# Expert results scattered to the tokens' order inside the expert loop, and one chunk of scans moved a layer on

## The reference

```python
logits = x @ router_w
expert_idx = jnp.argmax(logits, axis=-1)
score = jax.nn.sigmoid(jnp.max(logits, axis=-1))
xs = x * score[:, None]
for e in range(n_experts):          # 8 experts
    m = (expert_idx == e)[:, None]
    xe = jnp.where(m, xs, 0.0)
    h = jax.nn.silu(xe @ gate_w[e]) * (xe @ up_w[e])
    out = out + jnp.where(m, h @ down_w[e], 0.0)
shared = jax.nn.silu(x @ shared_gate_w) * (x @ shared_up_w) @ shared_down_w
return (out + shared)
```

## Time and profile before

| | us |
|---|---|
| median of 3 runs | 871.38 (870.98 to 872.09) |
| the profiled execution | 872.93 |
| its span, first to last instruction | 871.2 |
| TensorE busy | 758.9 (87%) |
| VectorE busy | 564.2 (65%) |
| ScalarE busy | 437.5 (50%) |
| GpSimd busy | 247.9 (28%) |
| mean granted clock of TensorE | 0.935 of full |

### The profile page before, as it was taken

One profiled execution on the slowest core, in us unless ns is written; L12 is line 12 of the kernel. 1 busy time (PEld: TensorE's weight loads), 2 busy tenths in 40 slices (PEclk: granted clock), 3 DMA queues, 4 the chain that ended last, 5 costly groups with the idle time before them and its releaser, 6 DMA issues.

```text
span 871.2 us, 11277 instructions
## 1 busy us (share of the span) xinstructions
PE 758.9 (87%) x3628; PEld 575.0 (66%) x3633; DVE 564.2 (65%) x1278; ACT 437.5 (50%) x878; POOL 247.9 (28%) x253
## 2 busy tenths in 40 slices
PE   0887787978865468899999999999998999999997
PEld 0433544634543137788888888888876788888885
DVE  5998898888897767656666666656664243223323
ACT  5895453234414765655555555545655244334342
POOL 5310112341440620202111111200123355555453
PEclk9999798789995867999999999999999999999999
DMA  4000002923322000210010110101011522313321
GB/s 154 2 2 1 0 0 84 407 66 113 99 67 79 1 0 1 98 49 28 22 50 1 49 51 1 37 1 38 1 49 42 155 61 86 89 31 85 85 56 48
DMA packets 37422, 49.84 MB, mean 57 GB/s; under 512 B 18574, under 2 KB 29942, under 8 KB 35702
## 3 DMA queue, kind: packets, MB, share of 16 engines
q1 hardware_dynamic: 36310, 46.90, 17.2%
q0 software_dynamic: 768, 2.10, 0.7%
q10 hardware_dynamic: 288, 0.14, 0.1%
HBM read 42.99 MB, written 6.13 MB: 56 GB/s over the span
## 4 chain that ended last, share of the span: by engine, by line
PE 57%; DVE 7%; ACT 2%; issue 1%; POOL 1%; DVEq 0%; ACTq 0%; POOLq 0%
PE bank L2058 15%; PE bank L2635 9%; PE bank L2074 8%; PE bank L2650 5%; PE bank L2630 5%; PE bank L2709 3%; PE bank L2726 3%; PE bank L2716 2%; PE bank L2708 1%; PE bank L2727 1%; PE bank L1774 1%; PE bank L1698 1%; POOL H L1485 1%; PE bank L1671 1%; DVE PN L2532 1%
## 5 line engine op out<-in xcount | busy, mean ns | idle before, releaser
L2102 DVE TENSOR_TENSOR B_l<-bank,TW_l 128x512 f32<-128x512 f32 (+1 forms) x50 | 34.5, 690 | 134.8 <-PE bank L2058 134.8
L2269 POOL TENSOR_TENSOR WL<-RAW,WH 128x512 fp32r<-128x512 f32 x28 | 35.8, 1281 | 222.4 <-ACT WH L2302 222.4
L2127 POOL TENSOR_TENSOR HL_l<-H_l,HH_l 128x512 fp32r<-128x512 f32 (+1 forms) x50 | 64.8, 1296 | 112.4 <-ACT HH_l L2119 112.4
L2361 ACT ACTIVATE EX<-EX,nm 128x128 f32<-128x128 f32 (+1 forms) x128 | 57.0, 446 | 67.1 <-DVE nm L2523 67.1
L2111 ACT ACTIVATE S_l<-bank 128x512 f32<-128x512 f32 (+1 forms) x50 | 29.9, 597 | 86.7 <-PE bank L2058 86.6
L2537 DVE TENSOR_TENSOR AL<-bank,AH 128x256 fp32r<-128x256 f32 x64 | 26.9, 423 | 53.9 <-ACT AH L2375 53.9
L2635 PE MATMUL bank<-XH,WH 128*128 128x512 f32 x128 | 58.6, 458 | 0.7 <-DVE XL L1823 0.7
L2058 PE MATMUL bank<-XH,WH 128*128 128x512 f32 (+1 forms) x136 | 54.5, 401 | 0.0
L2058 PE MATMUL bank<-XL,WH 128*128 128x512 f32 (+1 forms) x136 | 54.0, 397 | 0.0
L2058 PE MATMUL bank<-XH,WL 128*128 128x512 f32 (+1 forms) x136 | 54.0, 397 | 0.0
L2119 ACT ACTIVATE HH_l<-H_l 128x512 fp32r<-128x512 f32 (+1 forms) x50 | 31.6, 632 | 38.1 <-PE bank L2074 30.5
(11 more groups left out here) (328 smaller groups left out, 2202.5 us busy)
## 6 DMA issues: line engine op xcount, KB each, us to landing
RAW<-l_attn SPq DMA_DIRECT2D x8, 1024.0 KB, 4.8
WE<-l_experts SPq DMA_DIRECT2D x1, 6144.0 KB
TW_l<-routed SPq DMA_DIRECT2D x14, 256.0 KB, 4.1
RAW<-l_w SPq DMA_DIRECT2D x3, 1024.0 KB
RAW<-l_experts SPq DMA_DIRECT2D x6, 512.0 KB, 3.9
TW_l<-routed SPq DMA_DIRECT2D x14, 192.0 KB, 3.2
sorted_x<-ZERO SPq DMA_DIRECT2D x1, 1920.0 KB, 8.0
XIN<-sorted_x SPq DMA_DIRECT2D x15, 128.0 KB, 2.2
```

The source lines that it names most:

```text
L2127: pool.tensor_tensor(self.HL[0:rows, q % 4], self.H[0:rows, q % 2], self.HH[0:rows, q % 4].bitcast(F32), ALU.subtract).then_inc(self.h_low, 1)
L2361: act.activation(EX[:, s, a:b], EX[:, s, a:b], ACT.Exp, bias=nm[:, s, i:i + 1], scale=scale, accum_out=rs[:, s, i:i + 1]).then_inc(expd, 1)
```

## The change

- Each token's row in `sorted_x` gets a 257th column with the token's number, coded so that with the slot's own number it gives the row of the result in token order; an empty slot gives a row behind the tokens. For it TensorE computes each partition's number by one matmul (`number`), VectorE PART and BASE before its additions of chunk 8, and the column behind SLOT.
- SP loads that column for all 15 tiles (IDS, behind the third tile); VectorE makes indices of it after the third product.
- GpSimd scatters each tile's result straight to token order (`token_y`), between its gain work, in the order written out. SP's 15 stores and GpSimd's eight gathers are gone; SP loads the eight blocks of YG plainly once all scatters have landed.
- In tiles 3 and 8 the rounding of weights stands ahead of the gain piece. The third matrix's factors, scale and cap move behind the loop; ScalarE does the scale.
- The last three pieces (chunk 15's `den`, `num`, `add`) move behind `factors(1)` in the third layer.

```diff
-LOGITS1, RANKS1, START1, FETCH1, MIDDLE1, END1 = 2, 1, 5, 2, 15, 6
+LOGITS1, RANKS1, START1, FETCH1, MIDDLE1, END1 = 2, 1, 5, 2, 15, 3
...
-        XTOK = sb("XTOK1", [P, NT, D], F32)
+        XTOK = sb("XTOK1", [P, NT, D + 1], F32)
...
-        xs_d = nc.dram_tensor("sorted_x", (TILES1 * P, D), F32).ap()
-        ys_d = nc.dram_tensor("sorted_y", (TILES1 * P, D), F32).ap()
+        xs_d = nc.dram_tensor("sorted_x", (TILES1 * P, D + 1), F32).ap()
+        ys_d = nc.dram_tensor("token_y", (T + TILES1 * P, D), F32).ap()
...
@@ block.sync
-                sp.dma_start(XIN[:, j % RING1], xs_d[j * P:(j + 1) * P]).then_inc(x_in[j % RING1], 16)
+                sp.dma_start(XIN[:, j % RING1], xs_d[j * P:(j + 1) * P, 0:D]).then_inc(x_in[j % RING1], 16)
             for j in range(2 * RING1):
                 load(j)
+                if j == RING1 - 1:
+                    sp.dma_start(IDS[:].rearrange("p (j o) -> p j o", o=1),
+                                 xs_d[:, D:D + 1].rearrange("(j p) o -> p j o", p=P),
+                                 allow_slow_non_contiguous=True).then_inc(ids_in, 16)
             for j in range(TILES1):
                 if j + 2 * RING1 < TILES1:
                     load(j + 2 * RING1)
-                sp.wait_ge(y, j + 1)
-                sp.dma_start(ys_d[j * P:(j + 1) * P], YO[:, j % RING1]).then_inc(y_out[j % RING1], 16)
...
+            for n in range(RING1):
+                sp.wait_ge(y_out[n], 16 * len(range(n, TILES1, RING1)))
+            sp.wait_ge(absd, 3)
+            for t in range(NT):
+                sp.dma_start(YG[:, t, 0:D], ys_d[t * P:(t + 1) * P]).then_inc(y_in[t], 16)
@@ block.gpsimd
+            pool.wait_ge(home, 1)
...
-            for c in range(FIRST_GAIN1 + 1, LAYERS * NCH):
-                gain_pool(pool, k, c)
-                if c in OWN_NUM:
-                    gain_pool_num(pool, k, c)
-            for n in range(RING1):
-                pool.wait_ge(y_out[n], 16 * len(range(n, TILES1, RING1)))
-            pool.wait_ge(absd, 3)
-            for t in range(NT):
-                pool.indirect_dma_start(YG[:, t], None, ys_d, bass.IndirectOffsetOnAxis(ap=SLOT[:, t:t + 1], axis=0)
-                                        ).then_inc(y_in[t], 16)
+            def results(lo, hi):
+                for j in range(lo, hi):
+                    pool.wait_ge(goal, 2)
+                    pool.wait_ge(y, j + 1)
+                    pool.indirect_dma_start(ys_d, bass.IndirectOffsetOnAxis(ap=IDX[:, j:j + 1], axis=0),
+                                            YO[:, j % RING1], None).then_inc(y_out[j % RING1], 16)
+            own_term(9)
+            numerator(9)
+            own_term(10)
+            numerator(10)
+            own_term(11)
+            results(0, 2)
+            numerator(11)
+            own_term(12)
+            results(2, 6)
+            numerator(12)
+            own_term(13)
+            results(6, 10)
+            numerator(13)
+            own_term(14)
+            results(10, TILES1)
+            own_term(15)
@@ block.scalar
             result(TILES1 - 1)
+            act.wait_ge(factor, 6)
+            act.activation(RAW[:], RAW[:], ACT.Copy, bias=ROUND, scale=k.SW2[:, 2:3]).then_inc(rounded, 1)
             keep(2)
@@ block.vector
             v.tensor_tensor(HOT[:], KEY[:], each(kmax[:]), ALU.is_equal).then_inc(rt, 1)
+            v.wait_ge(part, 1)
+            v.tensor_scalar(PART[:], number, float(T), 1.0 / P, ALU.add, ALU.mult).then_inc(base, 1)
+            v.wait_ge(base, 1)
+            v.tensor_scalar(BASE[:], TILE[:, :, 0], PART[:, 0:1], float(P), ALU.add, ALU.mult).then_inc(base, 1)
             gain_pieces_done(v, k, PIECES[at:at + RANKS1])
...
             v.tensor_copy(SLOT[:], place[:]).then_inc(pos, 1)
+            v.wait_ge(base, 2)
+            v.scalar_tensor_tensor(XTOK[:, :, D], BASE[:, 0:NT], -2.0 * T, place[:], ALU.add, ALU.subtract).then_inc(home, 1)
...
                 v.tensor_tensor(HT[j % 3], ST[j % 3], up_banks[j % 3][:, F1:2 * F1], ALU.mult).then_inc(h, 1)
-                gain_pieces_done(v, k, pieces_after(j))
-                for m in range(3):
+                if j == 2:
+                    v.wait_ge(ids_in, 16)
+                    v.tensor_tensor(GOAL[:], IDS[:], BASE[:], ALU.add).then_inc(goal, 1)
+                    v.wait_ge(goal, 1)
+                    v.tensor_copy(IDX[:], GOAL[:]).then_inc(goal, 1)
+                for m in range(2):
                     if j == mean_tile(m):
+                        weight_factor(m)
...
+                        weight_cap(m)
+                gain_pieces_done(v, k, pieces_after(j))
-            gain_pieces_done(v, k, PIECES[FIRST_PIECE2 - END1:FIRST_PIECE2])
+            weight_factor(2)
+            tail = PIECES[FIRST_PIECE2 - END1:FIRST_PIECE2]
+            gain_pieces_done(v, k, tail[:1])
+            weight_cap(2)
+            gain_pieces_done(v, k, tail[1:])
@@ block.tensor
             mm.then_inc(turned, 1)
+            pe.wait_ge(consts, E1 + 3)
+            pe.matmul(number, BEFORE[:], ALL[:, 0:1], start=True, stop=True).then_inc(part, 1)
...
             pe.wait_ge(ws_in, 16)
+            pe.wait_ge(base, 1)
             shared_up(0)
...
@@ layer2, vector
             factors(1)
+            gain_pieces_done(v, k, PIECES[FIRST_PIECE2:-1])
```

More of the change, by code:

```diff
@@ L999, in layer1 @@
         ONE8 = sb("ONE81", [P, E1], F32)
-        ZERO = sb("ZERO1", [P, D], F32)
+        ZERO = sb("ZERO1", [P, D + 1], F32)
         top = sb("top1", [P, NT], F32)
@@ L1016, in layer1 @@
         EID = sb("EID1", [P, TILES1], mybir.dt.int32)
-        XTOK = sb("XTOK1", [P, NT, D], F32)
+        XTOK = sb("XTOK1", [P, NT, D + 1], F32)
+        PART = sb("PART1", [P, 1], F32)
+        BASE = sb("BASE1", [P, TILES1], F32)
+        IDS = sb("IDS1", [P, TILES1], F32)
+        GOAL = sb("GOAL1", [P, TILES1], F32)
+        IDX = sb("IDX1", [P, TILES1], mybir.dt.uint32)
         XIN = sb("XIN1", [P, RING1, D], F32)
@@ L1031, in layer1 @@
         RAW = sb("RAW2", [P, KD * FF2], F32)
-        xs_d = nc.dram_tensor("sorted_x", (TILES1 * P, D), F32).ap()
-        ys_d = nc.dram_tensor("sorted_y", (TILES1 * P, D), F32).ap()
+        xs_d = nc.dram_tensor("sorted_x", (TILES1 * P, D + 1), F32).ap()
+        ys_d = nc.dram_tensor("token_y", (T + TILES1 * P, D), F32).ap()
         cond = Cond("l1", sb, sem, residual=True, SG=SS)
         (r_in, ws_in, we_in, zeros, zeroed, made, consts, logits, turned, rt, sc, xtok, hot_sum, pos, scat, xt_turned, xt,
-         s_up, s_silu, s_h, up, silu, h, h_turned, hf, down, y, acc_sum) = [sem(n + "_1") for n in """r_in ws_in we_in zeros zeroed made
+         s_up, s_silu, s_h, up, silu, h, h_turned, hf, down, y, acc_sum, part, base, home, ids_in,
+         goal) = [sem(n + "_1") for n in """r_in ws_in we_in zeros zeroed made
             consts logits turned route score xtok hot_sum pos scat xt_turned xt s_up s_silu s_h up silu h h_turned hf down y
-            acc_sum""".split()]
+            acc_sum part base home ids_in goal""".split()]
         (raw_in, absd, wmean, factor, rounded, tern) = [sem(n + "_1") for n in "raw_in absd wmean factor rounded tern".split()]
@@ L1047, in layer1 @@
         total = banks[7][:, NT * E1:(NT + 1) * E1]
+        number = banks[5][:, 0:1]
         up_banks = (banks[0], banks[1], banks[7])
@@ L1065, in _ @@
             sp.dma_start(xs_d.rearrange("(j p) d -> p j d", p=P),
-                         ZERO[:].rearrange("p (o d) -> p o d", o=1).to_broadcast([P, TILES1, D])).then_inc(zeroed, 16)
+                         ZERO[:].rearrange("p (o d) -> p o d", o=1).to_broadcast([P, TILES1, D + 1])).then_inc(zeroed, 16)
             sp.dma_start(WS[:], io["l1_experts"][0]).then_inc(ws_in, 16)
@@ L1115, in _, with own_term, numerator @@
                                         None).then_inc(scat, 16)
-            for c in range(FIRST_GAIN1 + 1, LAYERS * NCH):
+            def own_term(c):
                 gain_pool(pool, k, c)
-                if c in OWN_NUM:
-                    gain_pool_num(pool, k, c)
-            for n in range(RING1):
-                pool.wait_ge(y_out[n], 16 * len(range(n, TILES1, RING1)))
-            pool.wait_ge(absd, 3)
-            for t in range(NT):
-                pool.indirect_dma_start(YG[:, t], None, ys_d, bass.IndirectOffsetOnAxis(ap=SLOT[:, t:t + 1], axis=0)
-                                        ).then_inc(y_in[t], 16)
+            def numerator(c):
+                gain_pool_num(pool, k, c)
+            def results(lo, hi):
[20 more added lines that the diff above has]
+            own_term(15)
         @block.scalar
@@ L1136, in _ @@
             for t in range(NT):
-                act.activation(XTOK[:, t], banks[t // 2][:, (t % 2) * D:(t % 2 + 1) * D], ACT.Copy,
+                act.activation(XTOK[:, t, 0:D], banks[t // 2][:, (t % 2) * D:(t % 2 + 1) * D], ACT.Copy,
                                scale=score[:, t:t + 1]).then_inc(xtok, 1)
@@ L1187, in _ @@
                             act.wait_ge(absd, m)
```

(14 more changed lines are left out.)

7 lines of the change are left out of this document (removed).

## The result

The changed kernel takes **867.07 us** (median of 6 runs, 866.25 to 869.06), the kernel before 871.74 beside it (6 runs, 870.27 to 872.70): ratio 0.995, interval 0.9936 to 0.9965. Forecast were 865.6 us, a range of 862 to 871, and faster. The profiled execution took 866.25 us (span 864.3), against 872.93 (span 871.2). It is the fastest of the changed kernel's six, and that of the kernel before is slower than all of its six, so the two profiles lie 6.7 us apart where the medians lie 4.7.

What follows compares the result with a forecast made beforehand. The prediction took VectorE as nearly the bound in the expert loop and the front as a chain. Its terms, +2.6 - 10.35 + 1.95 = -5.8 us, took the median from 871.38 to 865.6, range 862 to 871.

Steps and rivals of the forecast that it cites:

- signs of being wrong: VectorE waiting for identities or GpSimd's additions, a result waiting for its scatter before the last two tiles, YG matmuls awaiting loads.
- Step 1: Front: the gain additions wait for `number` behind the transposes, so `need`, scatters and first tile come later, +2.6 us.
- Step 2: Rows of 1028 bytes cost nothing, bounds 0 and +1.5 us; the identity load takes 3.4 us, covered.
- Step 3: Expert loop: moved rounding and shorter waits bring the last product from 243.28 to 236.8, -6.5 us.
- five waits: Expert loop before the change: 3.8 of VectorE's 6.0 us idle lie in five waits for ScalarE's ST.
- third rival: Expert loop closes up fully: last product at 233.2 to 234.5, time 862 to 863.3 us; chance 0.10.
- first rival: Expert loop doesn't close up: last product at 240.8 in place of 236.8, time 869.6 us; chance 0.20.
- Step 4: Second layer's tail: no wait for transfers, so TensorE's last work ends at 253.4 in place of 263.75, 10.35 us earlier.
- only the last two are near it (scatter 11 lands at 240.2): End of the loop: of ScalarE's results waiting for the scatter three tiles back, only the last two come near waiting.
- Step 5: Seam of third and fourth layer: the twelve moved instructions delay the residual, +1.95 us, bounds +1.4 and +4.
- Starved scatters: Tail: five late scatters slow down; 2.8 us each reaches 263.75, 4 us each gives 877.4 us; chance 0.08.
- Plain loads hidden for nothing: Front and seam cost more (+1.5, +2), so the time ends within 0.2%, 869.6 to 873 us; chance 0.08.

Runs made afterwards that it cites:

- e8: The changed kernel run once more without an edit: 868.04 us, ratio 0.9954 to the kernel before.
- e1: The changed kernel with the one-column matmul for the token numbers moved ahead of the router's logits: 865.49 us, ratio 0.9927 to the kernel before.
- e5: e1 with the rows of the sorted tokens 1280 bytes apart, 1028 of them used: 864.47 us, ratio 0.9914 to the kernel before.
- e2: The changed kernel with seven result buffers in place of three: 864.55 us, ratio 0.9929 to the kernel before.
- e7: The kernel before with the loop edits alone and chunk 15's pieces moved to the third layer, stores and gathers kept: 867.67 us, ratio 0.9956.
- e6: The changed kernel with the edits of e5 and e2 together: 864.26 us, ratio 0.9918 to the kernel before.
- e9: The changed kernel with chunk 15's four denominator scans placed two and two ahead of the third layer's maxima: 873.00 us, ratio 0.9989 to the kernel before.
- e4: The kernel before with the expert loop's rounding edits alone, stores, gathers and chunk 15 as before: 864.95 us, ratio 0.9909.
- e11: e7 with the moved denominator scans placed two and two ahead of the third layer's maxima: 869.24 us, ratio 0.9966 to the kernel before.

## Why the prediction was right, and where it was off

The time was 1.5 us above the forecast. That is less than its own terms were off: two errors cancelled, which is luck. None of the signs of being wrong that it named came. The last product came at 236.94 (forecast 239.4), and the matmuls of YG ended at 256.51 (near 256).

- **Step 1, the front (+2.6): right in mechanism and size.** VectorE stood 2.28 behind `number`, the additions took 2.4 (forecast 2.5), the first scatter came at 167.39 (forecast 167.5) and the first tile at 182.35 (182.6). By the first product the delay was 1.9 (3.1 in e8's profile).
- **Step 2, longer rows (at nothing, bounds 0 and +1.5): the mis-sized term.** "10 us before the first scatter" looked only at the zeros. The 6 MB behind them on the queues end 3.6 us later (26.9 against 23.3), close to the scatters. Alone this costs 1.5 (e1 to e5, 36.18 to 34.67), the upper bound; here it lies under step 1. Identities: 3.4 forecast, 2.9 measured, covered.
- **Step 3, the loop: right sign, gain too small.** VectorE's work was forecast at 46.3 and measured at 45.9 from first to last product (46.29 in the window above, which reaches 0.36 us further). Of its idle time I left 3.6 us; 2.2 are left, with one wait for ST of 1.1. The "five waits" of 3.8 were misread: three more of 1.4 stand under the tile's other name, DF, so there had been eight of 5.2. So the loop took 48.1 us, forecast 49.9. The prediction had no term for the clock in the loop, which went from 0.93 to 1.00. The closing up is nearer to the third rival than to the first. No wait for the identities, as forecast.
- **Step 4, the tail: 3.0 us too short (16.6 from the last product to YG's end; 19.6 measured).** The step that failed is "only the last two are near it (scatter 11 lands at 240.2)". The place was right and the landing was not: scatters 10 and 11 left GpSimd at 237.91 and 239.31, and ScalarE went on 1.5 and 3.0 later, where I had put 1.4. The last result is 5.7 behind the last product in place of 3.7. Then a term was missing: the shared matmuls at 7.13, the duration from a stretch without such a pause, took 10.21 (that the two hang together is shown at e2). On the other side the matmuls of YG, forecast at 8 times 0.71, took 3.73: the 0.71 is that of a group of four which stands alone.
- **Step 5, the seam (+1.95): +2.0 in the profile, VectorE without a pause before the residual.** Between profiles of one kind (see e8) the move costs 1.8 to 3.1, so the mechanism and the size are right and the agreement to 0.05 is luck.
- **The sum.** Front 0.7 and loop 1.8 better, tail 3.0 worse, so the layer's matmuls end 7.2 earlier and not 7.75. In this pair of profiles the rest of the kernel, untouched, was another 1.7 faster, which no step had; by the medians the gain is 4.7, or 3.6 by e8's runs, for 5.8 forecast.
- **Rivals.** Starved scatters: the last waits for a scatter are real, but scatters took 0.95 to 1.49 and one 2.04, far from 2.8 each. "Plain loads hidden for nothing" did not come as it was told, for front and seam cost what was forecast. But compared with e7, scatters and loads as written bring nothing, which no rival said; the time fell by the loop edits.

## What to carry to other kernels

Before an operation goes ahead of a long transfer or into it, ask when the last transfer behind it on the queues ends, not when it does itself; and let the rows of a scratch tensor keep a round distance when a column is added (1280 bytes for 1028 here). When results leave through an indirect scatter, take enough buffers for the scatters' whole backlog: a pause of TensorE may be paid a second time in the matmuls behind it. An edit with several parts should be run part by part: here the part that gave it its name brought nothing measurable as written, and 5 to 6 us of the layer, in single profiles, once its own side effects in the front and the tail were mended.

## What was not expected of the hardware

- **Where rows begin.** 1.93 MB of zeros from one buffer: 8.0 us in rows of 1024 bytes, 11.0 to 11.2 at 1028, 8.5 and 9.2 (e5, e6) with 1028 bytes every 1280.
- **A scan beside GpSimd.** 0.66 becomes 2.01 to 2.75 us (e9), while GpSimd's two products take 5.03 together (4.65 in the changed kernel).
- **Who begins first.** VectorE's rounding of H takes 0.69 us when it begins 0.08 to 0.18 us ahead of GpSimd's product, and 2.71 to 2.75 when it begins 0.14 to 0.20 behind it; then the product takes 2.34 to 2.37 in place of 2.73 to 2.83. A tenth of a microsecond earlier or later decides on 2 us.
- **The clock in stretches that no edit touches.** The last matmuls of the program are the same in all kernels. Most take 0.39 us in e4 (its row at 859.54, above) and 0.63 in the changed kernel (its row at 858.07). From the fourth layer's first projection on, e4 is shorter by 2.6 us.

From the fourth layer's first projection to the end it is 528.1 to 529.0 us in eleven of the profiles, 525.5 in e4 and 533.3 in e11. In e11's windows the loss is in the first 40 us, with a granted clock of 0.87 (1.00 in e7's):

```profile
336.57:376.57 40.00, 35.14 (x183) 30.31 (x183) 24.39 (x68) 20.97 (x51) 5.99 (x5) 0.87 0.17 59
```

So an execution may differ by 2 to 5 us in a stretch that no edit touches, as much as the gain of the whole change. This is why I read the layers' lengths beside the medians, and why it stays open whether e4's lower median is a gain of its code or of such stretches. Its two layers are 2.6 us longer than those of the changed kernel, but its profile is of the slowest of its six runs (866.80; the others 860.90 to 865.79), has the stretched rounding (2.0) and the slower stretch in the loop (1.7 against e7), while the changed kernel's is of its fastest.
